# Row-table stores with semaphores that outlive their stage, and gate scaling and accumulator clearing on GpSimd

## The chip, the cores and the metric

The kernel is one program on one core of a Trainium2 chip. The metric is its time on the device in microseconds (us), a median over runs. Six names are used below. PE is TensorE, which multiplies matrices, and PEld its weight loads. DVE is VectorE, ACT is ScalarE and POOL is GpSimd. SP is SyncE, which here issues most of the transfers (DMAs) and computes nothing. SPq is SP's instruction queue.

## The reference

Two layers of a graph network run over N = 3125 nodes with 256 features and E = 50000 edges that are sorted by destination. Cut to what matters here:

```python
xn = layernorm(x)
x = x + gnn0(xn, src, dst) + mix0(xn)      # layer 0: one attention head
x = x + ffn0(layernorm(x))                 # 8 experts, the best two of each node
xn = layernorm(x)
x = x + gnn1(xn, src, dst) + mix1(xn)      # layer 1: 8 heads
x = x + ffn1(layernorm(x))

# gnn: for each edge, the row of its source node, weighted, summed at its destination
ft = xn @ W;  a1, a2 = scores of each node
e = leaky_relu(a1[src] + a2[dst]);  p = exp(e - bound[dst])
out[n] = sum over edges into n of p * ft[src]  /  sum over edges into n of p

# mix1: linear attention times a gate
gate = sigmoid(gelu((xn * g + b) @ Wg1 + bg1) @ Wg2 + bg2)
```

In layer 1 the node rows come from rows that are normalised twice; the second normalisation is a factor `rho` for each node, which is put on the gate's inputs.

## The kernel before

The program is a chain of stages. A stage (`Stage`) owns its buffers and semaphores. Inside it a block gives every engine its own list of instructions; at the block's end all engines meet, and at the stage's end the semaphores are cleared and all engines meet again (L84, L85). Nodes lie in 25 tiles of 125 rows, edges in 98 blocks of 512.

The order of the stages is this. `first_tables` sorts and counts edges, normalises x and makes the node rows of layer 0. ACT lays them into `m.acc`, and SP stores them in five pairs of DMAs (L2231, L2232) to `table1` in DRAM. SP then waits until all ten have landed (L235). A short second block, `order_edges`, follows in the same stage; it loads two flags on each engine and has nothing to do for edges that are in order. `edge_sums` for layer 0 comes next (names with `es_`, called es0 here), then `graph_attention0`, then the first experts stage (`ffn0`) with `Combine` at its end. `Combine` adds the experts' rows to x, normalises, and makes the node rows of layer 1 (`table8`, 264 columns). For each tile it keeps 72 more columns in `m.tail`: 8 scores and 64 gate inputs. The trace calls `m.tail` kT, because it lies in that buffer. SP again waits for all ten stores (L1136). Then follow `edge_sums` for layer 1 (es1) with `Mix1` at its side, `finish1`, and the second experts stage.

Both edge stages work alike. POOL gathers the source rows of a block with four indirect DMAs of 128 rows (L683) into a ring of 8 slots; when it has filled all 8, it waits until a slot is freed (L672). SP counts what has landed (L669), and ACT waits for that count before it marks a block as ready (L778). The other engines work in 122 steps. In a step DVE compares edge ends with node numbers (L816), PE turns that mask (L722) and looks scores up (L711), DVE forms the edge score (L846 to L852), ACT the exponential (L753), DVE weights the rows (L826) and PE sums them (L703). DVE adds the sums to `m.acc` (L809). The mixer `side` puts its own instructions between, by the number of the step.

In es1, before the first step, POOL can start gathering at once. PE first needs `mix_zeros` and the scaled gate inputs, which DVE makes in its first pass (L2115, L2118). PE turns them in groups (L1988), and ACT applies the gelu (L2072), all before the first mask is turned (L722). DVE clears `m.acc` in its first five passes (L856). ACT starts on the gelu once `split` is set, with the last of DVE's three pieces of `adm` (L797).

Of the kernel before, what the change touches and what calls it, by code (L numbers as in the profile page):

```python
# [13 lines left out]
ALU = mybir.AluOpType  # L14
# [5 lines left out]
P, NT = 125, 25  # L20
D = 256
# [15 lines left out]
STEPS = NBLK + NT - 1  # L37
HALF = NBLK // 2
assert NBLK == 2 * HALF
TILE, BLK, SLOT, DONE = range(4)  # L40
LANDED, LAST = range(2)
SLOTS = 8
# [130 lines left out]
def first_tables(nc, m, src, dst, x, w, jobs, jobs_in):  # L173
# [7 lines left out]
    with Stage(nc) as c:  # L181
# [3 lines left out]
        def sem(n):  # L185
            return c.sem(n)
# [41 lines left out]
        normed, added, turned_x, staged, rowed, row_kept, moved, own_set, rows_out, edges_in, shifted_set = [  # L228
            sem("nt0_" + n) for n in ("normed", "added", "turned", "staged", "rowed", "row_kept", "moved", "own_set", "rows_out",
                                      "edges_in", "shifted")]  # L230
        table = m.table[1].rearrange("(t p) w -> p t w", p=P)
        ident_set, bias_set, ones_set, signed = [sem("edge_" + n) for n in ("ident_set", "bias_set", "ones_set", "signed")]
# [2 lines left out]
        with nc.Block() as block:  # L235
# [20 lines left out]
            @block.sync  # L256
            def _(sp):
                copy_rows(sp, ends[:, 1, :], dst.rearrange("(p c) -> p c", c=EC), loaded)
                copy_rows(sp, ends[:, 0, :], src.rearrange("(p c) -> p c", c=EC), loaded)
                sp.wait_ge(last_set, 1)  # L260
                sp.dma_start(next_first[0:P - 1, :], dst.rearrange("(p c) -> p c", c=EC)[1:P, 0:1]).then_inc(loaded, 16)
                for i in (2, 3, 4):
                    copy_rows(sp, m.xs[:, i * C:(i + 1) * C, :], x_rows[:, i * C:(i + 1) * C, :], x_in[i])
                sp.wait_ge(joined, 2)
                copy_rows(sp, m.edges[0:E, :].rearrange("(p c) x -> p c x", c=EC), pairs[:, :, :], stored)
                sp.wait_ge(setup, 4)
                sp.dma_start(m.edges[E:E + PAD, :].rearrange("(p c) x -> p c x", p=128), pad[:, :, :]).then_inc(stored, 16)
                sp.wait_ge(stored, 48)
                load_edges(sp, m, edges_in)
                for to, of in jobs:  # L270
                    sp.dma_start(to, of).then_inc(jobs_in, 16)
                for i in range(NT // C):
                    sp.wait_ge(own_set, i + 1)
                    copy_rows(sp, table[:, i * C:(i + 1) * C, :], m.acc[:, i * C:(i + 1) * C, 0:table_width(1)], rows_out)
                sp.wait_ge(rows_out, 32 * (NT // C))

            @block.gpsimd
            def _(pool):
# [314 lines left out]
def edge_sums(nc, m, tag, H, side_of=None):  # L593
# [4 lines left out]
    W = table_width(H)  # L598
    LOAD = 8
    LATE = 4  # L600
    OWN = 5
    with Stage(nc) as c:
        def sb(n, s, d=F32):
            return c.enter_context(nc.sbuf_tensor(tag + n, s, d))
# [56 lines left out]
        with nc.Block() as block:  # L661
# [11 lines left out]

            @block.gpsimd
            def _(pool):
                for q in range(NBLK):
                    if q == R:
                        bounds.gpsimd(pool)
                    if q >= R:
                        pool.wait_ge(freed, q - R + 1)  # L680
                    for w in range(BW):
                        at = (q * BW + w) * 2
                        pool.indirect_dma_start(rows[:, q % R, w, :], None, m.table[H],  # L683
                                                bass.IndirectOffsetOnAxis(ap=m.eall[:, at:at + 1], axis=0)).then_inc(gathered[q % R], 16)
# [50 lines left out]
            def _(a):  # L735
                tile_of, landed_of = column(a, m.steps, TILE, 0, NT - 1), column(a, m.counts, LANDED, 1, NBLK)
                a.activation(ends, m.ends[:, :], ACT.Copy).then_inc(ends_set, 1)
                if H == 1:
                    a.wait_ge(self_zed, 1)
                    a.activation(self_e[:, :, :], self_z[:, :, :], ACT.Exp).then_inc(self_exped, 1)  # L740
                    a.wait_ge(self_exped, 1)
                a.wait_ge(split, 1)

                def expose(p):
# [36 lines left out]
            def _(v):  # L781
# [49 lines left out]
                for i in range(STEPS + 5):  # L831
# [20 lines left out]
                        v.tensor_scalar(zq, zq, 0.0, None, ALU.min).then_inc(zed, 1)  # L852
                    if valid(p5):
                        add(p5)
                    if H > 1 and OWN * i < NT:
                        v.memset(m.acc[:, OWN * i:min(OWN * (i + 1), NT), 0:W], 0.0).then_inc(own_in, OWN)  # L856
                    side.vector(v, i)
                    if valid(p3):
                        weigh(p3)
# [158 lines left out]
def experts(nc, m, tag, gb, W1, b1, W2, b2, weighted, jobs, out, follow=None):  # L1018
# [8 lines left out]
    with Stage(nc) as c:  # L1027
# [108 lines left out]
        with nc.Block() as block:  # L1136
# [37 lines left out]
            def _(pool):  # L1174
# [29 lines left out]
                for j in range(NB):  # L1204
                    if j + SX < NB:
                        gather(j + SX)
                    scatter(j)

            @block.tensor
            def _(pe):  # L1210
# [258 lines left out]
class Combine:  # L1469
# [8 lines left out]
    def __init__(self, nc, m, c, halves, room, jobs_in, loads):  # L1478
        def sb(n, s, d=F32):
            return c.enter_context(nc.sbuf_tensor("ct1_" + n, s, d))  # L1480

        def sem(n):
            return c.sem("ct1_" + n)

        self.nc, self.m, self.halves, self.jobs_in, self.loads = nc, m, halves, jobs_in, loads
        self.pr = sb("pr", [128, D])
        self.half, self.other, self.shifted, self.shift = [sb(n, [P, NT]) for n in ("half", "other", "shifted", "shift")]
        self.bits = sb("bits", [P, NT], I32)
        self.xn = room.rearrange("p (s d) -> p s d", d=D)
        self.yy_in = [sem(f"yy_in{u}") for u in range(NT // self.C)]  # L1490
        (self.first, self.shifted_set, self.used, self.counted, self.chain, self.normed, self.turned, self.staged, self.rowed,
         self.row_kept, self.stored, self.biased, self.scaled) = [
            sem(n) for n in ("first", "shifted", "used", "counted", "chain", "normed", "turned", "staged", "rowed", "row_kept", "stored",
                             "biased", "scaled")]
        self.links = None

    def sync(self, sp):
        m, C = self.m, self.C
        table = m.table[HEADS].rearrange("(t p) w -> p t w", p=P)

        def load(u):
            for x in range(2):
                copy_rows(sp, self.halves(u, x), m.yrows[x * N:(x + 1) * N, :].rearrange("(p t) d -> p t d", p=P)[:, u * C:(u + 1) * C, :],
                          self.yy_in[u])

        def store(u):
            sp.wait_ge(self.row_kept, (u + 1) * C)
            copy_rows(sp, table[:, u * C:(u + 1) * C, :], m.acc[:, u * C:(u + 1) * C, 0:table_width(HEADS)], self.stored)
# [31 lines left out]
    def vector(self, v):  # L1540
# [100 lines left out]
class Mix0:  # L1641
# [55 lines left out]

    def output(self, i, late=0):
        return due(i - late, self.HIDDEN + 18, 1, 1)

    def tensor(self, pe, i):
        m, kv, W = self.m, self.kv, self.W
# [226 lines left out]
class Mix1:  # L1929
# [12 lines left out]
    def __init__(self, nc, m, c):  # L1942
        def sb(n, s, d=F32):
# [13 lines left out]
        self.bias = sb("bias", [128, KD])  # L1957
        names = ["zeroed", "made", "kept", "topped", "chain", "exped", "turned", "ekept", "summed", "levelled", "flipped", "flat",
                 "crossed", "mixer", "mapped", "ready", "qturned", "qkept", "queried", "bent", "gone", "out", "based", "added",
                 "gated", "zturned", "gate_bent"]  # L1960
        self.groups = [range(i, min(i + self.GROUP, NT)) for i in range(0, NT, self.GROUP)]
        (self.zeroed, self.made, self.kept, self.topped, self.chain, self.exped, self.turned, self.ekept, self.summed, self.levelled,
         self.flipped, self.flat, self.crossed, self.mixer, self.mapped, self.ready, self.qturned, self.qkept, self.queried,
         self.bent, self.gone, self.out, self.based, self.added, self.gated, self.zturned, self.gate_bent) = [
            c.sem("mix1_" + n) for n in names]

    def key(self, i, late=0):
# [5 lines left out]
    def output(self, i, late=0):  # L1973
        return due(i - late, self.OUT, 2, 1)

    def tensor(self, pe, i):
# [134 lines left out]
    def vector(self, v, i):  # L2111
        m = self.m
        if i == 0:
            self.links = Chain(v, self.chain, 0)
            v.memset(self.zeros[:, :], 0.0).then_inc(self.zeroed, 1)  # L2115
            self.links.link(v.tensor_scalar(self.bias[:, :], m.bg2[:, :], 0.5, None, ALU.mult))
            gates = m.tail[:, :, HEADS:]
            v.tensor_tensor(gates, gates, m.rho[:, :].unsqueeze(2).to_broadcast([P, NT, D // 4]), ALU.mult).then_inc(self.gated, 1)  # L2118
# [270 lines left out]
def program(nc, w, out):  # L2389
    m = Memory()  # L2390
    m.edges = nc.dram_tensor("edge_list", [E + PAD, 2], I32).ap()
    m.table = {H: nc.dram_tensor(f"table{H}", [N, table_width(H)], F32).ap() for H in (1, HEADS)}
    m.xrows = nc.dram_tensor("xrows", [N, D], F32).ap()
    m.yrows = nc.dram_tensor("yrows", [2 * N + NB * ROWS, D], F32).ap()
    with ExitStack() as c:
# [69 lines left out]
```

## Time and profile before

| what | value |
|---|---|
| median of 3 runs | 1868.52 us (1864.76 to 1869.58) |
| the profiled execution's own time | 1869.52 us |
| its span, first to last instruction | 1867.8 us |
| PE, DVE, POOL, ACT busy | 81%, 62%, 54%, 35% of the span |
| es0, first to last gather start | 67.26 to 569.87 us |
| es1, first to last gather start | 1007.83 to 1499.40 us |

The rows of the next sections come from the profiled execution; their times count from the start of its span. A timeline row gives start, duration, engine, line, operation, output <- inputs, and in brackets the idle time before it and what ended it.

### The profile page before, as it was taken

What the parts mean: (1) busy time and instruction counts of PE and PEld (TensorE: products, weight loads), DVE (VectorE), ACT (ScalarE), POOL (GpSimd) and SP (SyncE); (2) the same over time, 40 slices, a digit from 0 to 9 for tenths busy, and PEclk for the clock granted to TensorE, in tenths of its full rate; (3) what the DMA queues carried; (4) which work ended last, traced back from release to release, by engine and by line L of the source; (5) the groups of instructions that cost most, each with busy time, mean ns of one, the idle gap of its engine ahead of it and who ended that gap; (6) DMA issues with size and microseconds to landing.
All of it is one profiled execution on the core that took longest, in us unless ns stands there. A gap on an engine that the chain in (4) does not pass through costs nothing. (4 is left out here: it accounts for less than half of the span.)

```text
span 1867.8 us, 33348 instructions
## 1 busy us (share of the span) xinstructions
PE 1521.4 (81%) x9468; PEld 1263.8 (68%) x9468; DVE 1155.1 (62%) x3311; ACT 657.8 (35%) x2160; POOL 1009.5 (54%) x1093
## 2 busy tenths in 40 slices
PE   4488888898898968999936886988888867899991
PEld 4355656687775657999923775766666646799991
DVE  7586767775686663221174887878888888521214
ACT  4432222234324553333324434543322326423230
POOL 4577775777771002555403777777777722255540
PEclk9698998899999989999967999999999995999995
DMA  7533333333331055666563344444343302677667
GB/s 143 146 106 106 106 103 83 106 107 108 106 107 29 1 187 175 211 214 215 167 158 98 109 110 109 109 110 110 108 110 110 108 16 85 215 209 216 208 191 216
DMA packets 148022, 244.17 MB, mean 131 GB/s; under 512 B 53398, under 2 KB 83397, under 8 KB 147587
## 3 DMA queue, kind: packets, MB, share of 16 engines
q0 software_dynamic: 48384, 134.19, 25.8%
q1 hardware_dynamic: 97335, 106.27, 19.5%
q10 hardware_dynamic: 2124, 1.54, 0.4%
q8 instruction: 85, 1.39, 0.3%
q14 instruction: 94, 0.77, 0.1%
HBM read 210.48 MB, written 31.21 MB: 129 GB/s over the span
## 5 line engine op out<-in xcount | busy, mean ns | idle before, releaser
L683 POOL DMA_INDIRECT es_rows<-table,eall x784 | 746.0, 952 | 336.8 <-issue 235.6
L703 PE MATMUL bank<-es_msg,es_one 128*125 128x264 f32 x976 | 254.9, 406 | 87.0 <-DVE es_msg L826 87.0
L703 PE MATMUL bank<-es_rows,es_won 128*125 x976 | 261.7, 414 | 70.2 <-DVE es_won L823 69.8
L766 ACT ACTIVATE es_oneT<-bank 125x512 bf16<-125x512 f32 x244 | 145.3, 596 | 372.7 <-PE bank L722 370.8
L703 PEld LDWEIGHTS bank<-es_msg,es_one 128*125 128x125 f32 x976 | 177.1, 191 | 123.3 <-DVE es_msg L826 95.8
L703 PEld LDWEIGHTS bank<-es_rows,es_won 128*125 128x125 f32 x976 | 185.0, 200 | 104.0 <-issue 76.7
L1407 DVE TENSOR_TENSOR xT<-bank,xT 128x256 f32<-128x256 f32 x112 | 47.6, 425 | 327.2 <-PE bank L1258 327.2
L1301 ACT ACTIVATE xT<-bank,ffn_b1s 128x128 f32<-128x128 f32 x448 | 128.1, 369 | 303.0 <-PE bank L1248 303.0
L1248 PE MATMUL bank<-ffn_xbT,ffn_w 128*128 128x128 f32 x1792 | 220.1, 276 | 0.0
L1258 PE MATMUL bank<-ffn_w,xT 128*128 x896 | 211.6, 379 | 0.0
L1248 PEld LDWEIGHTS bank<-ffn_xbT,ffn_w 128*128 128x128 f32 x1792 | 210.8, 193 | 0.1
L1197 POOL DMA_INDIRECT yrows<-xT,ffn_dst_i x112 | 110.6, 987 | 183.8 <-DVE xT L1407 183.8
L1258 PEld LDWEIGHTS bank<-ffn_w,xT 128*128 128x128 f32 x896 | 161.8, 190 | 17.4
L1192 POOL DMA_INDIRECT ffn_xb<-xrows,ffn_src_i x112 | 108.7, 970 | 112.1 <-DVE ffn_dst_i L1386 77.2
L816 DVE TENSOR_TENSOR es_one<-nodes,bank 128x500 bf16 (+1 forms) x244 | 162.8, 667 | 3.2 <-issue 2.1
L826 DVE TENSOR_TENSOR es_msg<-es_rows,bank 128x1024 f32<-128x1024 f32 x122 | 148.6, 1218 | 3.8 <-ACT bank L753 1.6
L846 DVE TENSOR_TENSOR es_z<-es_rows,es_near 128x4 f32<-128x4 f32 (+1 forms) x244 | 42.8, 175 | 152.1 <-ACTq L778 145.1
L809 DVE TENSOR_TENSOR acc<-acc,bank 125x258 f32 (+1 forms) x244 | 104.2, 427 | 8.2 <-PE bank L703 3.8
L722 PE MATMUL bank<-es_ident,es_one 128*125 128x128 bf16 x976 | 101.3, 227 | 1.6 <-DVE es_one L816 1.1
L722 PEld LDWEIGHTS bank<-es_ident,es_one 128*125 128x125 bf16 x976 | 88.2, 141 | 19.5 <-issue 15.6
L711 PEld LDWEIGHTS bank<-es_stage,es_oneT 125*128 125x128 bf16 x976 | 62.4, 99 | 43.4 <-issue 6.9
L823 DVE TENSOR_TENSOR es_won<-es_one,bank 128x500 f32<-128x500 bf16 x122 | 81.6, 669 | 13.0 <-ACT bank L749 12.7
(448 smaller groups left out, 2347.9 us busy)
## 6 DMA issues: line engine op xcount, KB each, us to landing
ffn_w<-in_L_ffn_W SPq DMA_DIRECT2D x112, 512.0 KB
es_rows<-table,eall POOLq DMA_INDIRECT x784
ffn_w<-yrows SPq DMA_DIRECT2D x16, 560.0 KB
ffn_w<-in_L_ffn_W SPq DMA_DIRECT2D x2, 4096.0 KB
xrows<-acc SPq DMA_DIRECT2D x10, 560.0 KB
table<-acc SPq DMA_DIRECT2D x5, 577.5 KB
table<-acc SPq DMA_DIRECT2D x5, 564.4 KB
xT<-yrows SPq DMA_DIRECT2D x4, 560.0 KB
```

Source lines behind the costliest of these rows:

```text
L683: pool.indirect_dma_start(rows[:, q % R, w, :], None, m.table[H], bass.IndirectOffsetOnAxis(ap=m.eall[:, at:at + 1], axis=0)).then_inc(gat ...
L703: ins = pe.matmul(sum_banks[p % 2][0:P, 0:W], left, right, start=(w == 0), stop=(w == BW - 1))
L722: ins = pe.matmul(at, flags, ident[:, :], start=True, stop=True)
L766: a.activation(oneT[:, p % 2, :], turn_bank[0:P, :], ACT.Copy).then_inc(kept, 1)
L809: v.tensor_tensor(acc, acc, sum_banks[p % 2][0:P, 0:W], ALU.add).then_inc(added, 1)
L816: v.tensor_tensor(one[:, p % O, :, :], nodes, own, ALU.is_equal).then_inc(marked, 1)
L826: v.tensor_tensor(msg[:, p % 2, :, 0:D].rearrange("p w (h x) -> p w h x", h=H), rows_of(p, 0, D).rearrange("p w (h x) -> p w h x", h=H), w ...
L1192: pool.indirect_dma_start(xb[:, j % SX, :], None, m.xrows, bass.IndirectOffsetOnAxis(ap=src_i[:, j:j + 1], axis=0)).then_inc(x_in[j % SX], 16)
L1197: pool.indirect_dma_start(m.yrows, bass.IndirectOffsetOnAxis(ap=dst_i[:, j:j + 1], axis=0), y[:, j % SY, :], None).then_inc(y_out[j % SY], 16)
L1248: ins = pe.matmul(hidden_banks[s][:, h * 128:(h + 1) * 128], w1[:, j % SW, k, h * 128:(h + 1) * 128], xbT[:, s, k, :], start=(k == 0), sto ...
L1258: ins = pe.matmul(out_banks[s][:, 0:D], hT[:, s, h, :], w2[:, bass.ds(e, 1), h, :].rearrange("p a d -> p (a d)"), start=(h == 0), stop=(h ...
L1301: ins = a.activation(hT[:, s, h, :], hidden_banks[s][:, h * 128:(h + 1) * 128], ACT.Gelu, bias=b1s[:, j % SW, h:h + 1])
```

## The change

The table stores of both layers signal semaphores that are allocated once for the whole program, one for each pair of DMAs (`m.table_in`). SP no longer waits for them at the end of `first_tables` and of ffn0. In place of that POOL waits for all five before its first gather, in both edge stages. ACT in es0 waits for them before it scales `m.acc` in place.

In `Combine` POOL gets work. Once DVE has made `rho` it multiplies the gate inputs, five tiles at a time, and clears the 256 feature columns of `m.acc` for the tiles whose store has landed, 20 of the 25. `mix_zeros` is cleared by POOL at the start of es1. On DVE in es1 two clearings are left, one of 160 columns at once and one of the last five tiles, after a wait for the last store; the scaling of the gates is gone.

```diff
@@ first_tables, sync
-                    copy_rows(sp, table[...], m.acc[...], rows_out)
-                sp.wait_ge(rows_out, 32 * (NT // C))
+                    copy_rows(sp, table[...], m.acc[...], m.table_in[1][i])
@@ edge_sums, gpsimd
             def _(pool):
+                side.gpsimd(pool)
+                for stored in m.table_in[H]:
+                    pool.wait_ge(stored, 32)
                 for q in range(NBLK):
@@ edge_sums, scalar (H == 1)
                     a.wait_ge(self_exped, 1)
+                    for stored in m.table_in[H]:
+                        a.wait_ge(stored, 32)
@@ edge_sums, vector
-                    if H > 1 and OWN * i < NT:
-                        v.memset(m.acc[:, OWN * i:min(OWN * (i + 1), NT), 0:W], 0.0).then_inc(own_in, OWN)
+                    if H > 1 and i == 0:
+                        v.memset(m.acc[:, 0:NT - OWN, D:W], 0.0).then_inc(own_in, NT - OWN)
+                    if H > 1 and i == 1:
+                        v.wait_ge(m.table_in[H][-1], 32)
+                        v.memset(m.acc[:, NT - OWN:NT, 0:W], 0.0).then_inc(own_in, OWN)
@@ experts, gpsimd
                     scatter(j)
+                if after is not None:
+                    after.gpsimd(pool)
@@ Combine
-            copy_rows(sp, table[...], m.acc[...], self.stored)
+            copy_rows(sp, table[...], m.acc[...], m.table_in[HEADS][u])
-        sp.wait_ge(self.stored, 32 * (NT // C))
+
+    def gpsimd(self, pool):
+        m, C = self.m, self.C
+        pool.wait_ge(self.rho_set, 1)
+        for u in range(NT // C):
+            if u >= 1:
+                pool.wait_ge(m.table_in[HEADS][u - 1], 32)
+                pool.memset(m.acc[:, (u - 1) * C:u * C, 0:D], 0.0)
+            pool.wait_ge(self.row_kept, (u + 1) * C)
+            gates = m.tail[:, u * C:(u + 1) * C, HEADS:]
+            pool.tensor_tensor(gates, gates, m.rho[...].to_broadcast([P, C, D // 4]), ALU.mult)
@@ Combine, vector, after rho
+        v.sem_inc(self.rho_set, 1)
@@ Mix1
+    def gpsimd(self, pool):
+        pool.memset(self.zeros[:, :], 0.0).then_inc(self.zeroed, 1)
-            pe.wait_ge(self.gated, 1)
-            v.memset(self.zeros[:, :], 0.0).then_inc(self.zeroed, 1)
-            gates = m.tail[:, :, HEADS:]
-            v.tensor_tensor(gates, gates, m.rho[:, :]...to_broadcast([P, NT, D // 4]), ALU.mult).then_inc(self.gated, 1)
```

Two engines get another order. POOL, at the border between ffn0 and es1, before: the last scatters of ffn0, the two meetings, and the first 32 gathers.

```order
L1197 DMA yrows<-xT,ffn_dst_i 13418x256 x5
L1136 UNCONDITIONAL_BRANCH
L84 ISA
L674 UNCONDITIONAL_BRANCH
L683 DMA es_rows<-table,eall 128x264 x32
```

POOL at the same border with the change (the last of five multiplications and four clearings that now stand between the scatters and the meeting; lines have moved, L685 is the gather):

```order
L1532 MEMSET acc 125x5x256
L1535 TENSOR_TENSOR kT<-kT,w_rho 125x5x64
L1143 UNCONDITIONAL_BRANCH
L85 ISA
L673 UNCONDITIONAL_BRANCH
L2000 MEMSET mix_zeros 125x128
L685 DMA es_rows<-table,eall 128x264 x32
```

The gates' scaling and the clearing now stand ahead of the meeting, and one small clearing ahead of the first gather. DVE in its first two passes of es1, before (`es_one` is the mask of a step):

```order
L816 TENSOR_TENSOR es_one<-nodes,bank 128x500
L856 MEMSET acc 125x1320
L2115 MEMSET mix_zeros 125x128
L2116 TENSOR_SCALAR mix_bias<-w_bg 128x2
L2118 TENSOR_TENSOR kT<-kT,w_rho 125x25x64
L816 ISA
L816 TENSOR_TENSOR es_one<-nodes,bank 128x500
L856 MEMSET acc 125x1320
```

DVE at the same place with the change:

```order
L820 TENSOR_TENSOR es_one<-nodes,bank 128x500
L860 MEMSET acc 125x20x8
L2140 TENSOR_SCALAR mix_bias<-w_bg 128x2
L820 ISA
L820 TENSOR_TENSOR es_one<-nodes,bank 128x500
L863 MEMSET acc 125x1320
```

The large multiplication has left DVE, one of the two large clearings has become a small one, and three more that stood in the next passes are gone.

## Rows read from the trace of the kernel before

**Rows 1.** Page, costliest groups: engine, operation, count, busy us, mean ns, idle

```profile
L683 POOL DMA_INDIRECT es_rows<-table,eall x784 | 746.0, 952 | 336.8 <-issue 235.6
```

**Rows 2.** Waits of POOL in es1, 1000:1505: us in total, times, longest

```profile
POOL es_rows L683 <- issue: 118.5, 389, 0.3
...
POOL es_rows L683 <- SPq L672: 2.3, 2, 2.0
```

**Rows 3.** Timeline from the last store of table1 to es0's first gather

```profile
57.57 0.49 SPq L2232 DMA_DIRECT2D table<-acc  x1
...
61.15 0.27 DVE L410 CAST counts<-bank 1x128 uint16<-1x128 f32 x1
66.49 0.50 ACT L737 ACTIVATE bank<-ends 128x392 f32<-128x392 f32 x1 [9.69 <-PEq L85]
...
67.26 1.14 POOL L683 DMA_INDIRECT es_rows<-table,eall  x1 [15.21 <-POOLq L85]
```

**Rows 4.** SP's own waits over the whole span: us in total, times, longest

```profile
SPq L235 <- DMA table<-acc: 5.1, 1, 5.1
...
SPq L1136 <- DMA table<-acc: 3.2, 1, 3.2
```

**Rows 5.** Timeline from the end of Combine to es1's first gather

```profile
1001.53 0.23 ACT L1603 ACTIVATE kT<-bank 125x72 f32<-125x72 f32 x1
...
1001.86 0.27 DVE L1581 COPY adm<-kT 125x200 f32<-125x200 f32 x1 [12.13 <-ACT kT L1603]
1002.13 0.48 SPq L2232 DMA_DIRECT2D table<-acc  x1
1007.16 0.50 ACT L737 ACTIVATE bank<-ends 128x392 f32<-128x392 f32 x1 [5.41 <-PEq L85]
...
1007.83 0.99 POOL L683 DMA_INDIRECT es_rows<-table,eall  x1 [71.52 <-POOLq L85]
```

**Rows 6.** Timeline of Combine: the last step of rho, and the fourth store

```profile
989.54 0.19 DVE L2243 SCALAR_TENSOR_TENSOR w_rho<-ct_half,w_rho 125x25 f32<-125x25 f32 x1
...
996.02 0.48 SPq L2232 DMA_DIRECT2D table<-acc  x1
```

**Rows 7.** POOL's groups with their shapes: count, busy us, mean ns

```profile
L2191 POOL TENSOR_TENSOR acc<-acc,fin_rden 125x256 f32<-125x256 f32 x25 | 18.2, 766 | 34.9 <-DVE fin_rden L2211 34.9
...
L1187 POOL MEMSET ffn_zero<- 128x200 f32 x2 | 0.5, 256 | 0.0
```

**Rows 8.** Timeline of ffn1: POOL's first gather there and what it waits for

```profile
1612.93 0.22 DVE L1386 SCALAR_TENSOR_TENSOR ffn_dst_i<-ffn_holds,ffn_blank 128x56 int32<-128x56 f32 x1
1613.93 1.00 POOL L1192 DMA_INDIRECT ffn_xb<-xrows,ffn_src_i  x1 [38.72 <-DVE ffn_dst_i L1386]
```

**Rows 9.** Timeline of es1's start: two long gathers and the scaling of the gates

```profile
1014.14 1.05 POOL L683 DMA_INDIRECT es_rows<-table,eall  x1 [0.30 <-issue]
...
1019.32 1.83 DVE L2118 TENSOR_TENSOR kT<-kT,w_rho 125x1600 f32<-125x1600 f32 x1
1020.50 1.46 POOL L683 DMA_INDIRECT es_rows<-table,eall  x1 [0.30 <-issue]
```

**Rows 10.** Timeline of es1's start: split, the gelu, the first masks turned

```profile
1015.62 0.57 DVE L797 CAST es_parts<-es_msg 125x400 bf16<-125x400 f32 x1
...
1022.35 1.44 ACT L2072 ACTIVATE hgT<-bank,w_gate_bias 64x500 f32<-64x500 f32 x2 [14.68 <-PE bank L1988]
1024.16 2.87 ACT L2072 ACTIVATE hgT<-bank,w_gate_bias 64x500 f32<-64x500 f32 x5 [0.37 <-PE bank L1988]
...
1026.40 0.40 PE L722 MATMUL bank<-es_ident,es_one 128*125 128x128 bf16 x4
```

**Rows 11.** Waits of ACT in es1, 1110:1250: us in total, times, longest

```profile
ACT mix_slots L2087 <- SPq L669: 10.9, 7, 3.4
ACT kT L2079 <- SPq L669: 7.9, 4, 4.8
```

**Rows 12.** Timeline of DVE in es1: three of the 122 edge-score instructions

```profile
1245.44 0.19 DVE L846 TENSOR_TENSOR es_z<-es_rows,es_near 128x32 f32<-128x32 f32 x1 [1.24 <-ACTq L778]
...
1255.41 0.19 DVE L846 TENSOR_TENSOR es_z<-es_rows,es_near 128x32 f32<-128x32 f32 x1 [1.62 <-ACTq L778]
...
1280.51 0.19 DVE L846 TENSOR_TENSOR es_z<-es_rows,es_near 128x32 f32<-128x32 f32 x1 [1.10 <-ACTq L778]
```

More of the change, by code:

```diff
@@ L39 @@
 assert NBLK == 2 * HALF
+OWN = 5
 TILE, BLK, SLOT, DONE = range(4)
@@ L227, in first_tables @@
         xn = sb("nt0_xn", [P, 4, D])
-        normed, added, turned_x, staged, rowed, row_kept, moved, own_set, rows_out, edges_in, shifted_set = [
-            sem("nt0_" + n) for n in ("normed", "added", "turned", "staged", "rowed", "row_kept", "moved", "own_set", "rows_out",
+        normed, added, turned_x, staged, rowed, row_kept, moved, own_set, edges_in, shifted_set = [
+            sem("nt0_" + n) for n in ("normed", "added", "turned", "staged", "rowed", "row_kept", "moved", "own_set",
                                       "edges_in", "shifted")]
@@ L273, in _ @@
                     sp.wait_ge(own_set, i + 1)
-                    copy_rows(sp, table[:, i * C:(i + 1) * C, :], m.acc[:, i * C:(i + 1) * C, 0:table_width(1)], rows_out)
-                sp.wait_ge(rows_out, 32 * (NT // C))
+                    copy_rows(sp, table[:, i * C:(i + 1) * C, :], m.acc[:, i * C:(i + 1) * C, 0:table_width(1)], m.table_in[1][i])
             @block.gpsimd
@@ L600, in edge_sums @@
     LATE = 4
-    OWN = 5
     with Stage(nc) as c:
@@ L1491, in __init__ @@
         (self.first, self.shifted_set, self.used, self.counted, self.chain, self.normed, self.turned, self.staged, self.rowed,
-         self.row_kept, self.stored, self.biased, self.scaled) = [
-            sem(n) for n in ("first", "shifted", "used", "counted", "chain", "normed", "turned", "staged", "rowed", "row_kept", "stored",
+         self.row_kept, self.rho_set, self.biased, self.scaled) = [
+            sem(n) for n in ("first", "shifted", "used", "counted", "chain", "normed", "turned", "staged", "rowed", "row_kept", "rho_set",
                              "biased", "scaled")]
@@ L1507, in store @@
             sp.wait_ge(self.row_kept, (u + 1) * C)
-            copy_rows(sp, table[:, u * C:(u + 1) * C, :], m.acc[:, u * C:(u + 1) * C, 0:table_width(HEADS)], self.stored)
+            copy_rows(sp, table[:, u * C:(u + 1) * C, :], m.acc[:, u * C:(u + 1) * C, 0:table_width(HEADS)], m.table_in[HEADS][u])
         for u in range(NT // C - 1):
@@ L1515, in sync @@
             store(u)
-        sp.wait_ge(self.stored, 32 * (NT // C))
+    def gpsimd(self, pool):
[7 more added lines that the diff above has]
+            gates = m.tail[:, u * C:(u + 1) * C, HEADS:]
+            pool.tensor_tensor(gates, gates, m.rho[:, u * C:(u + 1) * C].unsqueeze(2).to_broadcast([P, C, D // 4]), ALU.mult)
     def fold(self, v, j):
@@ L1699, in output @@
         return due(i - late, self.HIDDEN + 18, 1, 1)
+    def gpsimd(self, pool):
+        pass
     def tensor(self, pe, i):
@@ L1959, in __init__ @@
                  "crossed", "mixer", "mapped", "ready", "qturned", "qkept", "queried", "bent", "gone", "out", "based", "added",
-                 "gated", "zturned", "gate_bent"]
+                 "zturned", "gate_bent"]
         self.groups = [range(i, min(i + self.GROUP, NT)) for i in range(0, NT, self.GROUP)]
@@ L1963, in __init__ @@
          self.flipped, self.flat, self.crossed, self.mixer, self.mapped, self.ready, self.qturned, self.qkept, self.queried,
-         self.bent, self.gone, self.out, self.based, self.added, self.gated, self.zturned, self.gate_bent) = [
+         self.bent, self.gone, self.out, self.based, self.added, self.zturned, self.gate_bent) = [
             c.sem("mix1_" + n) for n in names]
@@ L1974, in output, with gpsimd @@
         return due(i - late, self.OUT, 2, 1)
+    def gpsimd(self, pool):
+        pool.memset(self.zeros[:, :], 0.0).then_inc(self.zeroed, 1)
     def tensor(self, pe, i):
@@ L2114, in vector @@
             self.links = Chain(v, self.chain, 0)
-            v.memset(self.zeros[:, :], 0.0).then_inc(self.zeroed, 1)
             self.links.link(v.tensor_scalar(self.bias[:, :], m.bg2[:, :], 0.5, None, ALU.mult))
-            gates = m.tail[:, :, HEADS:]
-            v.tensor_tensor(gates, gates, m.rho[:, :].unsqueeze(2).to_broadcast([P, NT, D // 4]), ALU.mult).then_inc(self.gated, 1)
         k = self.links
@@ L2392, in program @@
     m.table = {H: nc.dram_tensor(f"table{H}", [N, table_width(H)], F32).ap() for H in (1, HEADS)}
+    m.table_in = {H: [nc.alloc_semaphore(f"table{H}_in{i}") for i in range(NT // OWN)] for H in (1, HEADS)}
     m.xrows = nc.dram_tensor("xrows", [N, D], F32).ap()
```

## The prediction

> **What bounds the kernel now.** I read the groups of the page first. The largest one on POOL is the gather of source rows: 784 of them, 392 in each edge stage, at 952 ns [rows 1]. The waits of POOL in es1 say what stands between them: 389 of 391 gaps are "issue", 118.5 us in total, 0.30 each, and only two gaps, 2.3 us, are a wait for a free slot [rows 2]. So a gather starts every 0.95 + 0.30 = 1.25 us, and a block of four lands every 5.0 us. POOL never rests until its ring is full.
>
> Next I asked who waits for whom inside es1. Between 1110 and 1250 ACT's waits end 14 times on SPq L669, the count of landed blocks, 18.8 us in these two groups [rows 11]. DVE's timeline shows the same a hop later: the edge scores start at 1245.44, 1255.41 and 1280.51, which lie 9.97 and 25.10 apart, two and five pitches of 5.0, each after a wait for ACT's mark (L778) [rows 12]. The last of these, at 1280.51, is the 62nd of 122; from there on DVE's, ACT's and PE's own work sets the pace and the gathers run ahead, which is why POOL at last meets a full ring. The reader is to see that a stage of this form is gather-bound in its first half and pipeline-bound in its second, and that the second half hangs on the last landed block of the first. **The end of es1 therefore moves with the start of its gathers, and with nothing that the other engines do before 1280.**
>
> So the borders count, where POOL does not gather. Ahead of es0 the timeline has the last store issued until 58.06, DVE's last instruction at 61.15 to 61.42, ACT's first of es0 at 66.49 and the first gather at 67.26 [rows 3]. SP's own wait for the stores is 5.1 us there, and 3.2 us at the end of Combine [rows 4]. Ahead of es1, ACT ends at 1001.76, DVE at 1002.13, the last store is issued until 1002.61, ACT starts es1 at 1007.16 and POOL gathers at 1007.83 [rows 5].
>
> **The change, part by part.**
>
> *Stores of layer 0.* SP is released at 58.06 + 5.1 = 63.16 and is last at the block's end. Without its wait the last there is DVE at 61.42, so all engines leave 63.16 − 61.42 = 1.7 us earlier. POOL's new wait costs nothing: the first gather would be due at 67.26 − 1.7 = 65.5, and the stores have landed by 63.16. The same holds for ACT's wait ahead of its scaling. If that cover were gone (stores still under way at 65.5), each us later would cost one. Bounds: 1.5 and 1.75, since rows of two engines are compared. I take **−1.7**, and it carries through es0 as a shift of the whole stage.
>
> *Stores of layer 1.* SP is released at 1002.61 + 3.2 = 1005.81, ACT starts 1.35 later and POOL 2.02 later [rows 5]. That POOL needs 0.67 more than ACT is its own way to a first gather. After the change the end of the block is set by whoever is last among ACT 1001.76, DVE 1002.13, SP 1002.61, and now POOL with its new list. POOL's list: `rho` is ready at 989.54 + 0.19 = 989.73 [rows 6]. A multiplication of 5 tiles is 5 × 64 = 320 elements per partition; 766 ns for 256 make 766 / 256 × 320 = 0.96 us. A clearing of 1280 elements is 256 / 200 × 1280 = 1.64 us at the rate of the small clearing, and 3.8 us at worst, at the rate of the multiplication [rows 7]. POOL's first four multiplications and three clearings have from 989.73 to the fourth store, which was issued until 996.50 [rows 6] and has landed 3.2 to 5.1 later, at 999.7 to 1001.6. The fourth clearing then ends between 1001.3 and 1005.4, the fifth multiplication waits for ACT's 1001.76 and ends between 1002.7 and 1006.4. I take 1002.8: SP's 1002.61 is as late, and 3.2 is the landing measured at this place. At the far end POOL itself would be later than SP is now, and the gain would be nothing.
>
> The stage then begins 1005.81 − 1002.8 = 3.0 us earlier; POOL could gather at 1007.83 − 3.0 = 1004.8, plus some 0.2 for clearing 128 columns of `mix_zeros`. But the last store has landed only at 1005.81, so POOL waits there. From the landing to the gather lies at least an issue gap of 0.30 [rows 2]; the nearest row is the first gather of ffn1, which starts 1613.93 − 1613.15 = 0.78 after the DVE instruction that it waits for [rows 8]. I take that: the first gather at 1006.6, **−1.2** against 1007.83. Bounds: 1005.81 + 0.30 gives −1.7, and POOL late or the wait as dear as today's 2.02 gives 0.
>
> *The scaling of the gates on DVE.* The gather at 1020.50 took 1.46 us, the one at 1014.14 took 1.05, and no other of es1's 392 is over 1.02. The long one began while DVE multiplied the gates, from 1019.32 to 1019.32 + 1.83 = 1021.15 [rows 9]. With that instruction gone I take 1.46 − 0.95 = **−0.5**; bounds 0 (another pair may collide instead) and −0.5. The Trainium skill ("SBUF — State Buffer", section "Who interferes with whom") infers that a tensor_tensor on DVE takes only the read side of the port that it shares with GpSimd and so leaves the writing of descriptors alone. By it this term would be 0 and the time 0.5 longer, 1865.6; the row is against it.
>
> *DVE's relief and the earlier pipeline.* DVE loses the 1.83 and four of five large clearings; ACT's split input, ready at 1015.62 + 0.57 = 1016.19, comes 2.9 earlier (1.7 aside), and the gelu no longer waits for the scaled gates. Today seven gelus of 2.87 or half of it start at 1022.35 and the first mask is turned at 1026.40 [rows 10]; then the gelu could start at about 1016.2 − 2.9 = 1013.3, nine us earlier. I cost this at nothing: the landing waits between 1110 and 1280 [rows 11, 12] hide it, because an earlier pipeline reaches the landed blocks earlier and waits longer. The cover would have to be gone for the nine us to count (rival A).
>
> *Added waits.* POOL's and ACT's waits on five semaphores are passed at once in es0. In es1 what is queued behind POOL's wait is the gathers (counted above); behind DVE's wait for the last store in its second pass nothing is late, as that pass runs after 1013, well behind 1005.81.
>
> Sum: −1.7 − 1.2 − 0.5 = −3.4. The profiled execution's own time is 1869.52, so it becomes 1866.1; that execution lies 1.00 above the median of the three runs, 1868.52, so the forecast is **1865.1**. The bounds together, −1.5 to −4.0, are 1864.5 to 1867.0.
>
> **The rivals.**
>
> *A: the head start counts.* If the pipeline did not fall back on landed blocks, es1 would end 9.0 earlier instead of 1.7: −1.7 − 9.0 = −10.7, 1857.8. For it: the nine us are real, and PE is 81% busy over the span. Against it: edge scores at landing times as late as 1280.51 [rows 12], 270 us after the head start.
>
> *B: the change does not do what it says in es1.* POOL's list ends late or the wait leaves POOL as slow as it is today, so the first gather stays where it is and another collision takes the place of the one removed. Only es0's 1.7 is left: 1866.8. For it: the last landing at 1005.81 is untouched by the change, and the far bounds of the clearing reach 1006.4. Against it: 0.78 in ffn1.
>
> *C: slower, through collisions.* DVE's instructions get another phase against the gathers, and long gathers become common: one such costs 0.51. If it hit every other of the 55 blocks gathered between 1008 and 1282, 27 × 0.51 = 13.8 us would be lost before the last landing-bound step, and the time would be 1865.1 + 13.8 = 1878.9. It decides from 18 collisions, 9.2 us, on, where 1865.1 passes 1874.1. Against it: the two pitches, 1.25 and about 4.4 to 5.0, drift through all phases today, and only two gathers of es1 are long [rows 9].
>
> **How the numbers follow.** About 0.3%, 5.6 us, is what a measurement of this kernel can tell from no change: faster is below 1862.9, slower above 1874.1. Chances: the forecast 0.70, A 0.10, B 0.16, C 0.04. The forecast and B both fall within 0.3%. I keep 0.10 of the forecast's share for runs that come out below 1862.9, since the three runs of before already reach from 1864.76 to 1869.58, and 0.01 of C stays under its threshold. So faster 0.10 + 0.10 = 0.20, same 0.77, slower 0.03. The range takes in the forecast's bounds and B, and on the lower side a part of the way to A, as a head start that is half kept would end there: 1861.0 to 1868.0. What is left out is A and C with some of the tails, under 2 in 10.
>
> **What would show it right or wrong.** Right: no wait of SP at the ends of first_tables and Combine; es0's first gather at about 65.5; ACT's first instruction of es1 some 3 us closer to the last store than today's 4.55, and the first gather 4.0 instead of 5.2 after the end of its issue; the first mask turned about nine us earlier; ACT's waits on landed blocks longer by about as much; edge scores still at landing times up to about the 62nd; no gather near 1.46 at es1's start. Wrong: the first gather of es1 as far behind the store as today (B); landing waits that end long before the 62nd step, or an es1 that is shorter by far more than its gathers began earlier (A); many gathers above 1.05 us (C); or POOL's clearings so slow that the meeting waits for it.

## The result and the profile after

Over nine runs each, the changed kernel takes 1872.61 us (1870.66 to 1878.3) and the one before 1866.91 us (1861.91 to 1869.58): the ratio is 1.0037, with a 95% interval of 1.0023 to 1.005. That is **slower by about 6.9 us** by the ratio; the two medians lie 5.7 apart. 1865.1 was forecast, 3.4 under the 1868.52 of the first three runs. The profiled execution took 1873.1 us, with a span of 1871.3.

The gathers are still the largest group on POOL, and one gather costs the same as in [rows 1]:

```profile
L685 POOL DMA_INDIRECT es_rows<-table,eall x784 | 745.0, 950 | 267.6 <-issue 251.3
```

At the first border (answering to [rows 3]) the step came out as forecast: 65.58 against the 65.5 of the text. By distance too: from the end of DVE's last instruction to the first gather it is 4.12 us, where it was 67.26 − 61.42 = 5.84. The timeline has

```profile
57.90 0.78 SPq L2254 DMA_DIRECT2D table<-acc  x1
...
61.19 0.27 DVE L410 CAST counts<-bank 1x128 uint16<-1x128 f32 x1
64.63 0.50 ACT L739 ACTIVATE bank<-ends 128x392 f32<-128x392 f32 x1 [8.51 <-PEq L86]
...
65.58 1.14 POOL L685 DMA_INDIRECT es_rows<-table,eall  x1 [14.20 <-issue]
```

At the second border (answering to [rows 5]) it did not. The timeline from the last piece of POOL's new work to the first gather of es1:

```profile
993.34 0.79 POOL L1535 TENSOR_TENSOR kT<-kT,w_rho 125x320 f32<-125x320 f32 x1 [0.87 <-ACT kT L1623]
993.63 0.48 SPq L2254 DMA_DIRECT2D table<-acc  x1
1004.47 0.21 POOL L2000 MEMSET mix_zeros<- 125x128 f32 x1 [10.34 <-POOLq L86]
1004.49 0.50 ACT L739 ACTIVATE bank<-ends 128x392 f32<-128x392 f32 x1 [11.23 <-PEq L86]
...
1005.37 1.02 POOL L685 DMA_INDIRECT es_rows<-table,eall  x1 [0.69 <-issue]
```

The last store is issued until 994.11, and POOL's last multiplication ends at 994.13. Then no engine computes for ten microseconds. From the end of the last store's issue to the first gather it is 11.26 us, where it was 5.22 in [rows 5] and 4.0 was forecast. The waits of SP in this stretch name PE's queue:

```profile
SPq L1143 <- PEq L1143: 9.2, 1, 9.2
```

But PE had been done since about 993. Here the name misleads: engines meet at L1143, and the view names whoever came to it last by its records. What each engine did at the meeting is seen when all instructions of that line are listed, those of the queues too (duration min/median/max in ns, then first and last start; the block occurs twice, in both experts stages):

```profile
L1143 POOLq EVENT_SEMAPHORE  x4: 17/17/17, 1003.4 to 1870.2; - x4
L1143 PEldq DRAIN  x2: 1303/1460/1617, 991.5 to 1827.2; - x2
L1143 ACTq DRAIN  x2: 541/855/1169, 992.8 to 1825.3; - x2
L1143 POOLq DRAIN  x2: 10046/10230/10414, 993.3 to 1829.4; - x2
L1143 DVEq DRAIN  x2: 283/370/458, 993.3 to 1865.1; - x2
L1143 SPq DRAIN  x2: 7/106/204, 994.2 to 1870.0; - x2
```

Each engine in this list ends the block with a DRAIN. PE, ACT, DVE and SP are done by 994.4. **POOL's DRAIN begins at 993.3 (the first of its two), lasts 10.05 us and ends at 1003.35**, 9.2 us after POOL's last instruction; POOL signals at 1003.4, and everybody leaves. The same view of the kernel before:

```profile
L1136 POOLq DRAIN  x2: 10419/10420/10421, 935.1 to 1828.1; - x2
```

It was there before as well, just as long, and ended at 945.5, 9.2 us after the last scatter's end at 936.31. It lay under Combine, which kept the other engines until 1005.81. The change gave POOL work at the end of Combine, and the drain, which stands behind POOL's last instruction, moved with it.

### The profile page after: what moved, and what is told of

It reads as the page before. It is cut to its first block and busy times, and to the rows that moved or that the text cites. A ratio compares the mean times of both kernels' runs of the same rounds, so it can differ in the third digit from the quotient of the medians.

```text
span 1871.3 us, 33359 instructions
## 1 busy us (share of the span) xinstructions
PE 1521.5 (81%) x9468; PEld 1262.9 (67%) x9468; DVE 1149.4 (61%) x3306; ACT 658.1 (35%) x2160; POOL 1016.7 (54%) x1103
## 5 line engine op out<-in xcount | busy, mean ns | idle before, releaser
L685 POOL DMA_INDIRECT es_rows<-table,eall x784 | 745.0, 950 | 267.6 <-issue 251.3
```

## The experiments

The theory is D: in the experts block POOL's drain takes 9.2 us from its last instruction on, and the change moved that instruction from 936 to 994 (66 us ahead of the end of the last store's issue in the trace of before, at its end in the changed kernel's). Rivals are W, that the amount of POOL's new work holds the meeting up; S, that the long-lived semaphores cost; and L or P, that the loss is in TensorE's clock in es1's second half. The first trace speaks for P too: in the second half of es1 the granted clock fell twice, and in the first trace of before it did not.

**e1_stores_only**: the changed kernel without POOL's work; DVE scales and clears in es1, as before (of DVE's lines only those that come back are shown).

```diff
@@ experts, gpsimd
-                if after is not None:
-                    after.gpsimd(pool)
@@ edge_sums, vector
+                    if H > 1 and OWN * i < NT:
+                        v.wait_ge(m.table_in[H][i], 32)
+                        v.memset(m.acc[:, OWN * i:min(OWN * (i + 1), NT), 0:W], 0.0).then_inc(own_in, OWN)
@@ Mix1, vector, i == 0
+            v.memset(self.zeros[:, :], 0.0).then_inc(self.zeroed, 1)
+            v.tensor_tensor(gates, gates, m.rho[:, :].unsqueeze(2).to_broadcast([P, NT, D // 4]), ALU.mult).then_inc(self.gated, 1)
```

> Only the store semaphores of both layers are kept from the change; DVE scales the gates and clears m.acc in es1 as before, and POOL has nothing to do in Combine. Theory D (POOL's drain at the end of the experts block holds it for 9.2 us after its last instruction, and the change moved that last instruction from 936 to 994): the drain lies under Combine again, so the first gather of es1 starts 3.5 to 4.0 us after the end of the last store's issue (before 5.22, with the change 11.26), and the kernel is 2.5 to 3.5 us faster than before (ratio 0.998). Rival S (the semaphores that outlive the stage cost the time themselves): the distance stays near 11 and the ratio near 1.004. Rival L (TensorE's clock falls in es1's second half, two in the changed kernel and none before, are what costs, and they come with the earlier start of es1): the distance is about 4, but the ratio is 1.000 or above.

Measured: 1862.33 us, ratio 0.9977 (0.9966 to 0.9988), **faster by 4.3 us**. The timeline:

```profile
997.89 0.48 SPq L2242 DMA_DIRECT2D table<-acc  x1
1002.41 0.99 POOL L685 DMA_INDIRECT es_rows<-table,eall  x1 [69.03 <-DMA table<-acc]
...
1011.83 1.82 DVE L2128 TENSOR_TENSOR kT<-kT,w_rho 125x1600 f32<-125x1600 f32 x1
1012.47 2.01 POOL L685 DMA_INDIRECT es_rows<-table,eall  x1 [0.30 <-issue]
```

The distance is 1002.41 − 998.37 = 4.04, and what the first gather waits for is now the store itself. S falls: the semaphores are all there, and the kernel is faster.

**e2_tiny_pool**: e1_stores_only with one column cleared on POOL.

```diff
@@ Combine
+    def gpsimd(self, pool):
+        pool.wait_ge(self.row_kept, NT)
+        pool.memset(self.spot[:, :], 0.0)        # 125 x 1, a buffer of its own
```

> As e1_stores_only, with one addition: POOL clears one column of a buffer of its own (125x1) after the last row of Combine is kept. Theory D: this instruction of about 0.1 us puts the whole drain of 9.2 us behind Combine, so the first gather starts 10.5 to 11 us after the end of the last store's issue, and the kernel is 6 to 7 us slower than e1_stores_only (ratio to before 1.002). Rival W (the amount of POOL's multiplications and clearings is what holds the meeting up): no difference from e1_stores_only.

Measured: 1869.21 us, ratio 1.0012 (1.0002 to 1.0021). The timeline, and the drain:

```profile
994.91 0.10 POOL L1527 MEMSET ct_spot<- 125x1 f32 x1 [64.27 <-ACT kT L1614]
995.23 0.48 SPq L2249 DMA_DIRECT2D table<-acc  x1
1006.22 0.99 POOL L685 DMA_INDIRECT es_rows<-table,eall  x1 [11.21 <-issue]
```

```profile
L1141 POOLq DRAIN  x2: 9332/9873/10414, 994.9 to 1826.8; - x2
```

An instruction of 0.10 us moves the gather from 4.04 to 10.51 us behind the store and costs 6.9 us (1869.21 − 1862.33). The drain ends at 994.9 + 9.33 = 1004.2, again 9.2 after the instruction's end. W falls: what counts is that POOL comes late, not how much it does.

**e3_early_drain**: the changed kernel with a drain where it is hidden.

```diff
@@ experts, gpsimd, behind the last scatter
                 if after is not None:
+                    pool.drain()
                     after.gpsimd(pool)
```

> The changed kernel with a drain of its own on POOL between its last scatter and its work in Combine. Theory D with a drain that clears up once what the indirect DMAs left behind: the early drain takes 9 us and is hidden, the one at the block's end takes under 1 us, the first gather starts about 4 us after the end of the last store's issue and the kernel is 2.5 to 3.5 us faster than before. Theory D with a drain that costs 9.2 us each time in this block: distance 11.3 as in the changed kernel, ratio 1.004. Rival W: distance 11.3 as well, with a short drain after late work.

Measured: 1864.45 us, ratio 0.9984 (0.9974 to 0.9994). One instruction more makes the changed kernel 8 to 10 us faster, by its two ratios, 1.0028 and 1.0037. The drains, the block's and the new one:

```profile
L1143 POOLq DRAIN  x2: 881/5646/10411, 994.9 to 1822.1; - x2
...
L1216 POOLq DRAIN  x1: 10419/10419/10419, 928.5 to 928.5; - x1
```

The early one takes the 10.42 us of the kernel before. The one at the block's end takes 0.88, of which 0.79 is the multiplication still running; the distance is 4.05. A drain clears up once.

**e4_before_again**: the kernel before, unchanged.

> The kernel before, once more, as a control: distance 5.2 from the end of the last store's issue to the first gather of es1, ratio 1.000 within 0.2%. If TensorE's clock falls in the second half of es1 depend on the program, none is seen there after 1285 as in the first trace; if they come by chance, one or two appear.

Measured: 1866.43 us, ratio 0.9997 (0.9986 to 1.0008). The distance is 1002.81 − 997.60 = 5.21, and the clock does not fall between 1285 and 1520. One more thing is read here: the last store ends its issue at 997.60, and at 1002.61 in the first trace of the same kernel. Positions on the time axis thus differ by 5 us between executions of one program, so distances are compared below. The long gather of [rows 9] is there again:

```profile
1014.39 1.83 DVE L2118 TENSOR_TENSOR kT<-kT,w_rho 125x1600 f32<-125x1600 f32 x1
...
1015.57 1.47 POOL L683 DMA_INDIRECT es_rows<-table,eall  x1 [0.30 <-issue]
```

**e5_dve_combine**: e1_stores_only with the gates scaled on DVE in Combine.

```diff
@@ Combine, vector, after rho
-        v.wait_ge(self.row_kept, NT)
+        for u in range(NT // C):
+            v.wait_ge(self.row_kept, (u + 1) * C)
+            gates = m.tail[:, u * C:(u + 1) * C, HEADS:]
+            k.link(v.tensor_tensor(gates, gates, m.rho[:, u * C:(u + 1) * C]..., ALU.mult))
```

> As e1_stores_only, but the gate inputs are scaled by DVE inside Combine, five tiles at a time as the rows are kept, while DVE waits there anyway; POOL has nothing to do in Combine. Theory D (only POOL's late drain costs): distance from the end of the last store's issue to the first gather about 4.0, no gather near 1.46 us at the start of es1, the first mask earlier than in e1_stores_only by some 4 us, and the time as e1_stores_only's within 2 us (the head start is lost at the landed blocks), so 2 to 5 us faster than before, ratio 0.998. Theory A (the pipeline's head start counts): 6 to 9 us faster than before, ratio 0.996.

Measured: 1862.95 us, ratio 0.9974 (0.9965 to 0.9984), distance 4.04, no gather over 1.03 at the start of es1. It beats both kernels, and its interval overlaps that of e1_stores_only. The earlier first mask did not come: PE's first work there still waits for `mix_zeros`, which DVE clears at 1011.61 in both. That part of the expectation was wrong.

**e6_es0_only**: the kernel before with the layer-0 semaphores alone (SP's wait at L235 gone, POOL and ACT wait in es0).

> The kernel before with the layer-0 part of the change alone: es0 starts 1.7 us earlier, the border ahead of es1 is as before (distance 5.2), so 1.7 us faster, ratio 0.999. If the gain of es0 is lost again inside es0 or behind it, ratio 1.000.

Measured: 1865.97 us, ratio 0.9998 (0.9986 to 1.001). The first gather of es0 is at 65.92, where it was at 67.26 and 68.43 in the two traces of before; the distance at the second border is 5.24. The 1.7 us lie within the interval, and so does nothing: inconclusive on the size in the time. At the border itself it is seen: from DVE's last instruction in `first_tables` to the first gather it is 4.11 (4.12 in the changed kernel), and was 5.84 and 6.82 in the two traces of before.

**e7_after_again** (the changed kernel once more) and **e8_padded** (e3_early_drain with five one-column clearings on DVE in es1, two in pass 0 and one in each of the passes 2 to 4, each into a column of its own) ask after the clock.

```diff
@@ Mix1, vector
+            v.memset(self.spot[:, 0:1], 0.0)
             self.links.link(v.tensor_scalar(self.bias[:, :], m.bg2[:, :], 0.5, None, ALU.mult))
+            v.memset(self.spot[:, 1:2], 0.0)
+        if 2 <= i <= 4:
+            v.memset(self.spot[:, i:i + 1], 0.0)
```

> The changed kernel once more. Theory P (TensorE's two clock falls in the second half of es1, at 1345 and 1475 in its first trace, come from places in the programs of ACT and DVE where an engine stands idle for 0.36 us with nothing to wait for): falls at the same two steps as in the first trace, the 79th to 81st and the 109th to 111th of 122. If they come by chance: at other steps, or none. Distance 11.3 and ratio 1.003 to 1.004 either way.

> As e3_early_drain, with five one-column clearings added to DVE's first passes of es1, so that DVE's program has as many instructions ahead of its later steps as before the change; they are done long before 1280 and cost nothing by themselves. Theory P: DVE's idle 0.36 us before the addition to m.acc, which stood at 1467.4 in e3_early_drain and is followed there by a fall of the clock, moves to another step (near 1233 as in the kernel before), no fall follows in the second half, and the kernel is about 2 us faster than e3_early_drain (ratio 0.9975). By chance: a fall near 1470 again, or anywhere, and the ratio stays at 0.9985.

Measured: e7_after_again 1871.31 us, ratio 1.0028 (1.0014 to 1.0042), distance 11.26; e8_padded 1864.69 us, ratio 0.9991 (0.9981 to 1.0), distance 4.05. What happens at the 109th step of es1 is seen in the changed kernel's first trace:

```profile
1474.50 0.43 DVE L813 TENSOR_TENSOR acc<-acc,bank 125x264 f32 x1 [0.36 <-issue]
...
1477.10 2.86 PE L705 MATMUL bank<-es_msg,es_one 128*125 128x264 f32 x8 [1.85 <-DVE es_msg L830]
```

and in its second, in e7_after_again:

```profile
1475.90 0.43 DVE L813 TENSOR_TENSOR acc<-acc,bank 125x264 f32 x1 [0.36 <-issue]
...
1478.51 2.04 PE L705 MATMUL bank<-es_msg,es_one 128*125 128x264 f32 x8 [1.83 <-DVE es_msg L830]
```

DVE stands idle for 0.36 us with nothing to wait for, at the same step in both; its weighted rows come late, and PE waits 1.83 to 1.85 instead of its usual 1.49. In the first trace the clock then falls from its upper level (2.4 GHz) to the lower (1.2 GHz): eight matmuls take 2.86 instead of 2.04. In the second it does not. A table of stretches (sums of busy time, then the granted clock, DMA share and GB/s) has for the first

```profile
1340.00:1350.00 10.00, 8.08 (x43) 5.98 (x42) 7.39 (x19) 2.38 (x10) 7.57 (x9) 0.83 0.40 106
...
1475.00:1485.00 10.00, 8.15 (x42) 6.26 (x41) 6.88 (x19) 2.22 (x8) 7.56 (x9) 0.83 0.41 109
```

and 1.00 for both in e7_after_again. (The fall of 1345 follows a wait of PE of 1.92, where the kernel's second trace has 1.86 and again no fall.) In e8_padded DVE's idle 0.36 lies at the 54th step, as in both traces of before, where the landed blocks hide it, and no fall follows in the second half:

```profile
1232.03 0.43 DVE L813 TENSOR_TENSOR acc<-acc,bank 125x264 f32 x1 [0.36 <-issue]
```

So P is half right. The place of DVE's idle time goes with the program; whether the clock falls there varies from execution to execution. Between 1290 and 1520 there are two falls in one trace of the changed kernel, none in the other, one in e3_early_drain, and none in the seven other traces of the table below, where PE never waits over 1.65. The two runs that follow, e9_drain_one_left and e10_drain_eight_left, have the changed kernel's es1: both show the same two waits (1.86 and 1.89, then 1.84 and 1.84), and each one fall, at the second. Over five traces the clock thus fell at the 109th step in four and at the earlier place in one. The idle time alone does not do it: in e1_stores_only and e2_tiny_pool such a gap of DVE stands at the 78th and 116th steps, where PE has the mixer's matmuls to do and no wait over 1.55, and the clock does not fall. e8_padded was expected 2 us faster than e3_early_drain and is not.

**e9_drain_one_left** and **e10_drain_eight_left** ask what sets the drain's length: the changed kernel with a drain of POOL's own ahead of its last scatter, or of the eighth from the end.

```diff
@@ experts, gpsimd, loop over blocks
+                    if after is not None and j == NB - 1:       # or NB - 8
+                        pool.drain()
                     scatter(j)
```

> The changed kernel with a drain of POOL's own ahead of its last scatter in the first experts stage, so that one indirect DMA lies between that drain and the one at the block's end. If a drain after any indirect DMA costs about 9.2 us: the drain at the block's end still lasts 10 us and the distance to the first gather is 11.3. If its length goes with what was issued since the last drain (112 indirect DMAs, 9.2 us: 0.08 each): the drain at the end lasts under 1.2 us, and the distance is 4 to 5. The new drain itself stands in the way of the last scatter and may cost some us ahead of Combine.

> As e9_drain_one_left, with eight scatters (and up to the same number of gathers) between POOL's own drain and the block's end. Fixed cost: 10 us again at the end. In proportion: 0.7 to 1.3 us of drain beyond the end of POOL's last instruction. In between (a cost that grows up to a limit): some us.

Measured, one run each: 1878.69 and 1879.46 us, since the new drain holds up the last scatters; the issue of the last store ends only at 1007.82 and 1009.95. Behind it the first gather comes after 4.03 us in both. The drain at the block's end in e9_drain_one_left, and in e10_drain_eight_left with the new one:

```profile
L1143 POOLq DRAIN  x2: 976/5696/10417, 1007.0 to 1836.4; - x2
```

```profile
L1143 POOLq DRAIN  x2: 1792/6103/10414, 1009.1 to 1836.4; - x2
L1215 POOLq DRAIN  x1: 10816/10816/10816, 906.7 to 906.7; - x1
```

Behind the end of POOL's last instruction (1007.83 and 1009.96) they last 0.15 and 0.93 us, with starts read to 0.1; of that some 0.08 are left even in e3_early_drain, where no indirect DMA lies between the two drains. In the second, 8 scatters and 3 gathers were issued since the drain before: 0.085 us each. The new drain ended at 917.5, 8.3 us after the last gather's end (909.22), for the 101 before it: 0.082 each. And 112 in 9.2 us are 0.082 each. In this block the drain costs 0.08 us per indirect DMA issued since the last drain, even when they landed long ago.

## Why the prediction was wrong

All traces beside each other, in us. "Border" is from the end of the last store's issue to es1's first gather; the next columns count from that gather to the 1st, the 76th and the 122nd edge score (the rows of [rows 12]).

| kernel | border | 1st | 76th | 122nd | ratio |
|---|---|---|---|---|---|
| before | 5.22 | 24.0 | 326.6 | 519.0 | 1 |
| e4_before_again | 5.21 | 23.7 | 326.3 | 518.6 | 0.9997 |
| changed | 11.26 | 18.1 | 325.8 | 522.4 | 1.0037 |
| e7_after_again | 11.26 | 18.1 | 326.0 | 519.1 | 1.0028 |
| e1_stores_only | 4.04 | 21.5 | 327.2 | 519.9 | 0.9977 |
| e2_tiny_pool | 10.51 | 23.9 | 326.7 | 519.3 | 1.0012 |
| e3_early_drain | 4.05 | 16.3 | 326.2 | 520.9 | 0.9984 |
| e5_dve_combine | 4.04 | 21.5 | 325.9 | 518.1 | 0.9974 |
| e6_es0_only | 5.24 | 23.9 | 326.9 | 519.2 | 0.9998 |
| e8_padded | 4.05 | 15.9 | 325.9 | 518.5 | 0.9991 |

**The step that failed** is the end of Combine's block: "The fourth clearing then ends between 1001.3 and 1005.4, the fifth multiplication waits for ACT's 1001.76 and ends between 1002.7 and 1006.4. I take 1002.8". POOL's list itself was sized well: it ended 0.02 us after SP's last issue, where 0.2 was forecast, with multiplications of 0.72 to 0.79 us (0.96 forecast) and clearings of 1.17 (1.64). But the end of its last instruction was taken for POOL's arrival at the meeting. Between them lie 9.2 us of drain. The term was −1.2 and measured 11.26 − 5.22 = **+6.0**. The outer bound, "the gain would be nothing", did not hold it either. The row was within reach: POOL's drain from 935.1 to 945.5 stood in the trace of before, but in no table of busy time, as it belongs to the queue. The prediction asks of its other terms what would be paid if the cover were gone; it did not ask this of POOL's end of block.

**Stores of layer 0, −1.7:** right at the border: 4.12 from DVE's last instruction to the gather, against 5.84, is −1.72, and −2.7 against the 6.82 of e4_before_again. e6_es0_only could not tell its size in the time.

**Wait for the last store:** right. Landing of 3.2 [rows 4] and 0.78 [rows 8] make 3.98 from the store to the gather; the kernels without a late drain show 4.04 and 4.05.

**The long gather, −0.5:** right for the pair of kernels. While DVE scales the gates in es1 a gather took 1.44 to 1.47 and, in e1_stores_only, 2.01 us; where DVE does not, none at es1's start is over 1.04. The traces show more: all 20 gathers of es1 above 1.03 us in the twelve traces began while DVE ran a tensor_tensor with both inputs in SBUF, and ended 0.80 to 0.83 us after that instruction. So its price goes with how early in DVE's instruction it begins: 0.64 us into it in e1_stores_only (2.01 us), 1.18 in the kernel before (1.46). The inference in the Trainium skill ("SBUF — State Buffer", section "Who interferes with whom") that a tensor_tensor on DVE leaves descriptor generation alone does not agree with these rows, if the gather's time is taken for the writing of its descriptors; what in the gather is held up no run here shows.

**The earlier pipeline, 0:** right, and the table shows it best. The first edge score comes 15.9 to 24.0 us after the first gather, the 76th always 325.8 to 327.2. Eight microseconds of head start are gone by then. The head start itself was real: the first mask is turned 14.9 us after the last store's issue in e3_early_drain and 23.8 in the kernel before, the nine us of the prediction; in the changed kernel the late drain took them back (23.9). Rival A falls with it, and e3_early_drain and e8_padded, with the largest head starts, are no faster than e1_stores_only.

**The sum:** −1.7 + 6.0 − 0.5 = 3.8. The two measurements of the changed kernel are 6.9 (4.3 to 9.3 by its interval) and 5.2 (2.6 to 7.8). So up to 3 us are left, for which the prediction had no term. Part of it lies between the 76th and the 122nd edge score. That stretch took 192.3 to 192.7 us in the seven traces without the two long waits of PE; with the waits and no fall of the clock 193.1 (e7_after_again); with one fall 194.7 to 194.9 (e3_early_drain, e9_drain_one_left, e10_drain_eight_left); with two 522.4 − 325.8 = 196.6 (the changed kernel's first trace). A fall thus costs 1.7 to 1.8, and over the five traces the stretch is 2.4 longer on average; as an estimate, that makes 3.8 + 2.4 = 6.2. Against it stands that e8_padded, without these waits, is not faster than e3_early_drain. A run without a profile shows its mean granted clock alone, not where it falls, so the split of the rest between the clock and the noise stays open.

Rival C had the right sign and the wrong mechanism: no long gathers became common. That the meeting could wait for POOL stood under what would make the prediction wrong, with slow clearings as the reason, and in rival B, which priced it at today's start of the gathers.

Two counts of the prediction are off by one, and nothing hangs on them: between 1110 and 1250 ACT's waits end 13 times on SPq L669, and the edge score at 1280.51 is the 63rd.

## What to carry to other kernels

Before an engine that has been idle at the end of a block is given work there, look at what its queue does after its last instruction, not only at the instruction: a drain that was hidden moves along. If POOL has issued many indirect DMAs, put a drain of its own where it is covered, or give the work to an engine whose drain is short. And ask of each stretch what pins its end: here es1's end hung on the start of the gathers, and everything that came earlier on other engines was lost at the landed blocks.

## What the runs showed of the hardware

POOL's DRAIN costs 0.08 us per indirect DMA issued since the last drain in the experts block (112: 9.2 us; 11: 0.93; 1: 0.15), whether it stands 0 or 64 us behind the last of them. In the edge stages it is shorter than that rate would make it: behind 392 gathers the drain of es1 in the kernel before (the second of the line, begun at 1495.4 and 8.60 long) ended about 3.65 us after the last one. Why is open.

```profile
L661 POOLq DRAIN  x2: 8599/13728/18856, 555.8 to 1495.4; - x2
```

A wait of PE in es1's second half that was longer by 0.34 to 0.43 us than the 1.49 of its neighbours stood in five traces, twice in each; five of the ten were followed by the lower clock (a granted clock of 0.83 over 10 us), at 1.7 to 1.8 us each. At one of the two places, where four of the five falls came, DVE had stood idle for 0.36 us; the position of that gap moves with the number of instructions ahead of it.
